# A GNN layer and a top-2 mixture of experts in one kernel: second dispatches deferred, slot loads paced, group 0 taken ahead in the opening

## What is computed

```python
def _L0_gnn_ref(x, adjacency, epsilon, W1, b1, rms_weight, W2, b2):
    neighbor_sum = jnp.einsum('bnm,bmd->bnd', adjacency, x)
    agg = epsilon * x + neighbor_sum
    h = jnp.einsum('bnd,dh->bnh', agg, W1) + b1          # H = 512
    h = jax.nn.silu(_rmsnorm(h, rms_weight))
    return jnp.einsum('bnh,hd->bnd', h, W2) + b2

def _L0_ffn_ref(x, Wg, bg, W1, b1, W2, b2):              # E = 8 experts, H = 512
    top_w, top_i = jax.lax.top_k(xf @ Wg + bg, 2)
    top_w = jax.nn.softmax(top_w, axis=-1)
    ...
    for e in range(E):
        h = jax.nn.gelu(xf @ W1[e] + b1[e], approximate=False)
        out = out + w_dense[:, e:e + 1] * (h @ W2[e] + b2[e])

x = x + _L0_gnn_ref(_layernorm(x), adj, ...)
x = x + _L0_ffn_ref(_layernorm(x), ...)
```

## Time and profile before

| | |
|---|---|
| runs | 565.95 us median (565.26 to 566.77) |
| profiled execution | 568.35 us, span 566.4 us, mean granted clock 0.934 |
| TensorE busy | 488.4 us (86%) |
| GpSimd busy | 361.7 us (64%) |
| VectorE busy | 354.4 us (63%) |
| ScalarE busy | 262.8 us (46%) |

### The profile page before, as it was taken

How to read it: one execution, slowest core, us unless ns; L and a number is a source line. 1 busy time by engine, 2 the same in 40 slices (tenths; PEclk the granted TensorE clock), 3 DMA queues, 4 the chain that set the end, 5 groups by cost and what they waited for, 6 DMA issues and landing times. The chain is left out here.

```text
span 566.4 us, 14003 instructions
## 1 busy us (share of the span) xinstructions
PE 488.4 (86%) x3693; PEld 437.6 (77%) x3693; DVE 354.4 (63%) x1486; ACT 262.8 (46%) x812; POOL 361.7 (64%) x334
## 2 busy tenths in 40 slices
PE   2589889999899998555718999999999999999993
PEld 1467677777677776455618999999999999999993
DVE  6647777666666766226424666767676767676762
ACT  0214123222222332114305777777777777777771
POOL 2323478887788786663473545454556888888886
PEclk9959789999998998977777999999999999999997
DMA  7971122222222221330122222322223555555531
GB/s 251 367 232 29 28 62 69 73 72 72 64 62 64 65 71 35 78 87 16 37 74 72 78 74 86 98 71 65 73 57 51 70 68 73 68 77 74 70 34 14
DMA packets 54577, 45.01 MB, mean 79 GB/s; under 512 B 9522, under 2 KB 46040, under 8 KB 54503
## 3 DMA queue, kind: packets, MB, share of 16 engines
q1 hardware_dynamic: 36480, 26.11, 16.9%
q0 software_dynamic: 16592, 17.13, 15.4%
q10 hardware_dynamic: 1430, 0.88, 0.6%
HBM read 25.75 MB, written 19.25 MB: 79 GB/s over the span
## 5 line engine op out<-in xcount | busy, mean ns | idle before, releaser
L663 ACT ACTIVATE gelu_t<-ps,block_w 128x128 f32<-128x128 f32 x568 | 163.0, 369 | 44.6 <-PE ps L566 25.4
L566 PE MATMUL ps<-slot_t,block_w 128*128 128x128 f32 x1136 | 154.8, 280 | 19.1 <-issue 13.7
L566 PEld LDWEIGHTS ps<-slot_t,block_w 128*128 128x128 f32 x1136 | 141.7, 196 | 20.6 <-issue 14.4
L376 POOL DMA_INDIRECT dispatched_rows<-payload,row_idx x128 | 127.0, 992 | 42.2 <-issue 35.7
L581 PE MATMUL ps<-experts,gelu_t 128*128 x1136 | 152.4, 278 | 0.5 <-ACT gelu_t L663 0.3
L581 PEld LDWEIGHTS ps<-experts,gelu_t 128*128 128x128 f32 x1136 | 140.1, 194 | 1.2 <-issue 1.1
L411 POOL DMA_INDIRECT out_y<-y_out,slot_rows x71 | 112.9, 1590 | 24.2 <-issue 21.3
L408 POOL DMA_INDIRECT out_y<-y_out,slot_rows x71 | 69.7, 982 | 66.2 <-issue 52.3
L942 DVE TENSOR_TENSOR y_bias<-ps,block_w 128x128 f32<-128x128 f32 x142 | 41.5, 292 | 98.3 <-issue 43.4
L930 DVE COPY block_w<-experts 128x644 f32 x142 | 71.1, 501 | 1.4 <-issue 1.3
L498 PE MATMUL ps<-w2e,hidden 128*128 128x136 f32 x512 | 71.8, 291 | 0.0
(11 more groups left out here) (135 smaller groups left out, 453.5 us busy)
## 6 DMA issues: line engine op xcount, KB each, us to landing
slot_rows<-dispatched_rows SPq DMA_DIRECT2D x142, 66.5 KB
xs<-in_x SPq DMA_DIRECT2D x16, 256.0 KB, 6.9
xs_t<-in_x_t SPq DMA_DIRECT2D x16, 256.0 KB, 7.1
experts<-in_f_w SPq DMA_DIRECT2D x16, 256.0 KB, 5.2
out_y<-y_out,slot_rows POOLq DMA_INDIRECT x142
adj_in<-in_adj_t SPq DMA_DIRECT2D x16, 128.0 KB, 6.3
dispatched_rows<-payload,row_idx POOLq DMA_INDIRECT x128
dispatched_rows<-pad_rows SPq DMA_DIRECT2D x18, 66.5 KB
```

Of the source, the lines that this page charges most:

```text
L376: pool.indirect_dma_start(rows[k], bass.IndirectOffsetOnAxis(row_idx[:, g, j * TOP_K + k:j * TOP_K + k + 1], 0), payload[:, g * JT + j, 0: ...
L566: mm = pe.matmul(bank((2 * i + c // 2) % FH_BANKS, c % 2 * SLOTS, SLOTS), block_w[:, i % BLOCKS, c * P:(c + 1) * P], slot_t[:, i % 2, :], ...
L663: act.activation(gelu_t[:, i % 2, c, :], ps[:, (2 * i + c // 2) % FH_BANKS, c % 2 * SLOTS:(c % 2 + 1) * SLOTS], ACT.Gelu, bias=block_w[:, ...
```

## The change

- GpSimd dispatches only the rows of the first expert (k = 0) in their step. Of the second expert's 64 dispatches, two a step follow one group later (`dispatch_second`), 30 in all; the other 34 stand between the first 60 tile writes. They have a semaphore of their own, for which SP waits before load 71.
- SP's first 16 slot loads wait for the 48 early k = 0 dispatches alone, and each for a mark of progress: of the last two groups (0 to 5) or of the slot norms (6 to 15). A pad follows each of the loads 16 to 31.
- TensorE's steps before 0 are written out anew: group 0's aggregation and quadratic form, the set-ups, spread(0), aggregate(2), and then step 0 with group 1's quadratic form and sums inside it, spread(1), quadratic(2) and sum_squares(2) behind it.
- In every step `prefix(s - 1)` moves behind the last `second_layer`.
- epsilon is the first load of ScalarE; a Silu on one column runs ahead of its loop; norm1(0) stands ahead of the W1 operations, setup_w2 behind scale_agg(0); the gate's set-up product uses PSUM bank 4 instead of 1.

```diff
@@ SP
+            def pad(g):
+                end = sp.value_load(region_end[0:1, g:g + 1], min_val=0, max_val=DUMMY - SLOTS)
+                sp.dma_start(rows[g // E][bass.ds(end, SLOTS), :], pad_rows[:]).then_inc(padded, 16)
...
-            sp.wait_ge(early_dispatched, 16 * JT * TOP_K * EARLY_GROUPS)
+            sp.wait_ge(early_dispatched, 16 * JT * EARLY_GROUPS)
             for i in range(RING):
+                if i < 4:
+                    sp.wait_ge((h_done, h_done, prefix_done, l2_done)[i],
+                               (C * (G - 2) + 1, C * (G - 1), G - 2, G - 1)[i])
+                elif i < 6:
+                    sp.wait_ge(h_done, (C * (G - 1) + 1, C * G)[i - 4])
+                else:
+                    sp.wait_ge(slots_normed, i - 5)
                 load_slots(i)
             sp.wait_ge(ends_ready, 1)
-            pad(0)
             for i in range(RING, EARLY):
                 load_slots(i)
-            pad(1)
+                if i - RING < KE:
+                    pad(i - RING)
...
-            sp.wait_ge(late_dispatched, 16 * JT * TOP_K * (G - EARLY_GROUPS))
-            for i in range(EARLY, NT):
+            sp.wait_ge(late_dispatched, 16 * JT * (G - EARLY_GROUPS))
+            for i in range(EARLY, TILES):
+                load_slots(i)
+            sp.wait_ge(second_dispatched, 16 * JT * G)
+            for i in range(TILES, NT):
                 load_slots(i)
@@ GpSimd
                 if live(s - 1):
                     pow_ln2(s - 1)
                 if live(s - 2):
-                    dispatch(s - 2, (0, 1))
+                    dispatch(s - 2, 0, 0)
+                    dispatch(s - 2, 1, 0)
+                if live(s - 3):
+                    dispatch_second(2 * (s - 3))
                 for g in STATS_AT.get(s, ()):
                     pow_ln1(g)
                 if live(s + 2):
                     pow_rms(s + 2)
                 if live(s - 2):
-                    dispatch(s - 2, (2, 3))
+                    dispatch(s - 2, 2, 0)
+                    dispatch(s - 2, 3, 0)
+                if live(s - 3):
+                    dispatch_second(2 * (s - 3) + 1)
             for i in range(NT):
...
+                write_tile(i)
+                done = 2 * (G - 1)
+                left, until = G * JT - done, TILES - 11
+                if i < until and (i + 1) * left // until > i * left // until:
+                    dispatch_second(done + i * left // until)
@@ TensorE
+            aggregate(0)
+            setup_quad()
+            quadratic(0)
+            aggregate(1)
+            setup_turns()
+            sum_squares(0)
+            setup_gate()
+            spread(0)
+            aggregate(2)
+            for s in range(G):
+                first_layer(s, (0, 1))
+                if s == 0:
+                    quadratic(1)
+                elif live(s + 1):
                     spread(s + 1)
+                first_layer(s, (2, 3))
+                if s > 0 and live(s + 2):
                     quadratic(s + 2)
...
+                residual(s, 0)
+                residual(s, 1)
+                second_layer(s, 0)
+                second_layer(s, 1)
+                if s == 0:
+                    sum_squares(1)
+                elif live(s + 2):
                     sum_squares(s + 2)
+                residual(s, 2)
+                second_layer(s, 2)
+                residual(s, 3)
+                second_layer(s, 3).then_inc(l2_done, 1)
                 if live(s - 1):
                     prefix(s - 1)
                 if live(s + 3):
                     aggregate(s + 3)
+                if s == 0:
+                    spread(1)
+                    quadratic(2)
+                    sum_squares(2)
@@ ScalarE
+            act.dma_start(eps_col[:], epsilon.to_broadcast([P, 1])).then_inc(eps_loaded, 16)
...
             act.wait_ge(pool_consts, 2)
+            act.activation(table_warm[:], ones[:, 0:1], ACT.Silu)
@@ VectorE, setup_w1
                 place_adj(0)
+                norm1(0)
                 dve.wait_ge(w1_loaded, 32)
```

More of the change, by code:

```diff
@@ L68, in moe_gnn @@
     AHEAD = 4
-    assert D == P and C == 4 and G > 8 and SLOTS == P
+    assert EARLY >= RING + KE and D == P and C == 4 and G > 8 and SLOTS == P
     with ExitStack() as ctx:
@@ L85, in moe_gnn @@
         before = sb("before", [P, P], BF16)
+        table_warm = sb("table_warm", [P, 1])
         neg_half = sb("neg_half", [P, JT])
@@ L370, in pow_rms, with dispatch, dispatch_second, write_tile @@
                                    ALU.pow).then_inc(rrms_ready, 1)
-            def dispatch(g, tiles):
-                pool.wait_ge(rows_ready, g + 1)
[L374 to L379, removed]
+            def dispatch(g, j, k):
+                if k == 1:
+                    signal = second_dispatched
+                else:
+                    signal = early_dispatched if g < EARLY_GROUPS else late_dispatched
+                pool.wait_ge(rows_ready, g + 1)
+                pool.indirect_dma_start(
+                    rows[k], bass.IndirectOffsetOnAxis(row_idx[:, g, j * TOP_K + k:j * TOP_K + k + 1], 0),
+                    payload[:, g * JT + j, 0:WID], None).then_inc(signal, 16)
+            def dispatch_second(n):
+                if n < G * JT:
+                    dispatch(n // JT, n % JT, 1)
+            def write_tile(i):
+                r = i % RING
+                pool.wait_ge(y_ready, i + 1)
+                token = bass.IndirectOffsetOnAxis(slot_rows[:, r, TOKEN:TOKEN + 1].bitcast(I32), 0)
+                if i < TILES:
+                    pool.indirect_dma_start(out, token, y_out[:, r, :], None, bounds_check=T - 1,
+                                            oob_is_err=False).then_inc(added[r], 16)
+                else:
+                    pool.indirect_dma_start(out, token, y_out[:, r, :], None, bounds_check=T - 1,
+                                            oob_is_err=False, compute_op=ALU.add).then_inc(added[r], 16)
             for s in range(-4, G + 2):
@@ L444, in setup_gate @@
                 for c in range(C):
-                    pe.matmul(bank(1, c * E, E), w2_t[:, c, :], ident_wg[:, P:ZW], start=True, stop=True)
-                pe.matmul(bank(1, C * E, E), b2_rows[:], ident_wg[:, P:ZW],
+                    pe.matmul(bank(4, c * E, E), w2_t[:, c, :], ident_wg[:, P:ZW], start=True, stop=True)
+                pe.matmul(bank(4, C * E, E), b2_rows[:], ident_wg[:, P:ZW],
                           start=True, stop=True).then_inc(setup_pe, 1)
@@ L518, in _ @@
             pe.matmul(bank(0, 0, H), ones[:], w1g, start=True, stop=True).then_inc(setup_pe, 1)
-            for s in range(-3, G):
-                if s == -2:
-                    setup_quad()
-                if live(s):
-                    if s == 0:
-                        pe.wait_ge(setup_dve, 9)
-                    first_layer(s, (0, 1))
-                if live(s + 1):
+            aggregate(0)
[3 more added lines that the diff above has]
+            setup_turns()
@@ L534, in _ @@
[L534 to L547 removed]
+                if s == 0:
+                    pe.wait_ge(setup_dve, 9)
@@ L898, in _ @@
             for s in range(-4, G):
-                if s == 0:
-                    setup_w2()
                 if live(s - 1):
                     second_norm(s - 1)
-                if live(s + 3):
+                if live(s + 3) and s > -3:
                     norm1(s + 3)
@@ L906, in _ @@
                     scale_agg(s + 1)
+                if s == -1:
+                    setup_w2()
                 if live(s - 1):
```

44 lines of the change are left out of this document (6 added, 38 removed).

## The result

The changed kernel is slower: 601.68 us median (600.93 to 602.0, 4 runs) against 566.36 (565.26 to 567.6, 4 runs) in the same session, a ratio of 1.062 [1.059, 1.065]. The profiled execution took 600.93 us, its span is 598.7.

The account below looks back on a forecast made before the run. GpSimd's queue was taken to bound the group loop and the accumulating writes. Terms 215.8 + 39 + 136.2 + 137.5 gave a span of 528.5 us, 37.9 less than 566.4; forecast 528 us, own range 517 to 540.

Parts of the forecast that it names:

- Writes and dispatches mixed: First part of tile loop: 71 writes and 34 dispatches fill GpSimd for 133.7 us, 2.0 us a tile at first.
- group 15's first layer: End of group loop: reached at 215.8 us instead of 232.17, by -11.4 for the loop and -5.0 for the opening.
- to the first tile write: From the last group's first layer until GpSimd starts tile writes: 39 us, bounds 34.6 and 55.5.
- to the first accumulating write: First half of tile writes with the moved dispatches between them: 136.2 us, set by GpSimd's own time.
- to the end: From the first accumulating write to the kernel's end: 137.5 us, as before, GpSimd issuing without a wait.
- The passage: Between group loop and tile loop: paced loads and fewer dispatches remove most stops, 39 us to GpSimd's first tile write.
- Opening: Before the steady group loop: group 3's first layer at 77 to 78 instead of 82.87, -5 us, bounds -9 and +2.
- Group loop: Ten group steps: 11.7 us each against 12.84 with fewer dispatches and moved prefix, -11.4 us, bounds -13 and -3.
- Load 71: Tile loop: SP's slot load waiting for the last dispatch lands some 4 us before its y is wanted.
- The lock of the two engines: Tile loop rival: dispatches wait for VectorE's block copies, 34 x 0.489 = 17 us, total 545 us; chance 0.03.
- Slower: Tile loop rival: dispatches stop the other engines, 1.43 us each, 49 us for 34, total 577 us; chance 0.06.
- The stops stay: Passage rival: stops come from engines' first pass through new code, 55.5 us instead of 39, total 545; chance 0.2.

Follow-up runs that it names:

- opening-and-prefix version: Kernel before with the new opening and moved prefix alone, GpSimd and SP as before: 560.18 us (0.989) on a slower chip, 526.3 us (0.994) on a faster one.
- session 3: Repeat of the unaltered changed kernel against the kernel before, on another slower chip: 597.43 us, ratio 1.057.
- paired version: Kernel before, nothing added, first-half tile writes in pairs 1.28 us apart: 530.14 us (1.001) on a faster chip, 578.47 us (1.023) on a slower one.

## Why the prediction was wrong

**What failed.** The step "Writes and dispatches mixed". It added up GpSimd's own time and put the price of a dispatch in the tile loop at its 1.26 us on GpSimd, nothing for the others. In the four terms of the sum:

| term, us | predicted | result (slower chip) | faster chip |
|---|---|---|---|
| group 15's first layer | 215.8 | 217.7 | 216.7 |
| to the first tile write | 39 | 43.9 | 36.3 |
| to the first accumulating write | 136.2 | 198.2 | 142.3 |
| to the end | 137.5 | 138.8 | 138.7 |
| span | 528.5 | 598.7 | 534.0 |

62.0 of the 70.2 us lie in the third term. That it is the moved dispatches is shown by the run with them back in the loop; that it is their being DMAs, by powers against 16-row writes on one chip. The forecast's description (GpSimd never waits, 2.0 us a tile) is what the faster chip shows, but not the chip the kernel was measured on, where the earlier trace rows already had the warning: all engines but GpSimd stand while GpSimd issues.

**The passage.** The size was near and within its bounds (43.9 for 39), for the wrong reason. I put the stops down to SP's loads and GpSimd's dispatches together and expected pacing of the loads to remove most. Pacing gained at most 2 us; spacing dispatches, with SP's burst kept, brought tile 10 forward by 18.6 (between two slower chips). On a faster chip the opening-and-prefix version has the burst too (16 loads in 17.39 us), and no idle over 4.17 us. What shortened the passage in the changed kernel is, by the nearest comparison, its fewer dispatches, six a step for eight: up to group 15's row_idx it differs from the version with all eight in the loop by nothing else, and from group 15's first layer to there lie 35.9 us (39.7 in session 3) against 46.0. That comparison is between chips. Whether SP's loads must be there at all for the stops was not tested.

**Opening.** Forecast -5 us at group 3's first layer, measured 82.87 - 74.07 = 8.8, inside the bound of 9. Spread(2) came at 49.40, not 53: 27.40 for first_layer(0) was 1.5 us early, and VectorE reached product(2) at 42.30, not 46.1. The term was mis-sized by 3.8 us.

**Group loop.** Forecast 11.7 us a step, measured 12.0, with the idle before the prefix gone. From group 4's to group 14's first layer: 208.93 - 86.11 = 122.8 against 128.4, so -5.6 and not -11.4, inside the bound of -3. Half of the shortfall of 5.8 us is 12.0 for 11.7 in nine steps (2.9 us): an idle of 0.32 us before the quadratic form, waiting for agg_r (the row at 102.48), which wasn't there before. The other half (3.0 us) is the step of 14.66, with a 2.27 us idle at the same place, in which VectorE makes the early table. The kernel before has that step too: its 12.84 us are a mean of nine steps of 12.66 and one of 14.48 (208.82 to 223.30), and the forecast took it away with the rest. The two errors, of opening and loop, nearly cancel: 217.7 for 215.8.

**Load 71.** I had it land 4 us before "its y is wanted". It is wanted earlier, by the norm four tiles ahead, and GpSimd reaches the last dispatch late. On the faster chip this idle of 7.96 us is more than the term's whole excess (6.1). I did name the idle as a sign of error, but gave it no price. On the slower chip it is hardly there, since all are late alike: load 71 goes at 434.56, 3.2 us after the last dispatch, and TensorE's longest idle between tiles 60 and 76 is 1.63 us.

**The lock of the two engines.** The Trainium skill, "SBUF - State Buffer", section "SBUF: two separate sides", would have a dispatch between tiles wait for a block copy. I weighed this with writes of 977 to 982 ns "beside" copies of 485 to 491 ns, and that reading was wrong: in the kernel before none of the 50 block copies between tiles 10 and 60 overlaps a write, so it says nothing. In the changed kernel 21 of 50 overlap a GpSimd DMA, and there the trace agrees with the page in kind: the copy at 320.64, beside the write at 320.02, takes 0.68 us, and dispatches take up to 1317 ns (median 961). The size is small, 0.58 us in the mean for an overlapping copy against 0.49. It is not the cause of the stops: on the faster chip all 50 copies overlap (up to 0.68 us), without them. The low chance was right, its evidence wasn't.

**The rivals.** "Slower" was right in its mechanism, its place and nearly in its price: 1.43 us a dispatch, measured 1.39 (16 rows, slower against faster chip), and 62.0 / 34 = 1.8 in the result with all else in that term. It was given 0.06, on the argument that a hundred dispatches in the group loop go with idles of 1 us. The observation was right, the conclusion wasn't: the changed kernel's ten steps with 60 dispatches take 122.8 and 121.2 us on slower chips and 121.1 on a faster one, and no silu, copy or product starts late there. With 80 dispatches the ten steps of the kernel before take 128.4 us, and those of its variants on faster chips 122.1 to 122.8: at most 0.08 us a dispatch. The price of 1.4 us belongs to the tile loop, and the stops to it and the passage. What these have and the group loop hasn't is open. One difference is SP's own DMAs: 13 in the 122.8 us of the ten steps, 60 in the 146.8 us between tiles 10 and 60. That 1.43 and 1.39 agree so closely is partly luck, as 1.43 was one stop divided by eight dispatches. "The stops stay" is true in part (it is small beside the rest), but not its mechanism: the same code runs without long stops on the faster chips, and spacing the dispatches removes most of them on a slower one.

**Why slower even on the faster chip.** The kernel before takes 529 us there, and its variants with an unchanged passage have no idle over 2.61 us in it, so the passage has little to give. The changed kernel reaches tile 0 at 235.1, 9.4 us ahead of the opening-and-prefix version (244.5). At tile 60 it is 3.6 ahead, since GpSimd sets 2.0 us a tile for 1.9, and at tile 71 it is 7.6 behind, through load 71.

**What stays open.** Why a GpSimd DMA makes other engines start late on some chips and not on others, and in the tile loop but not in the group loop. The DMAs' own times, their rows and bytes are ruled out as the difference; what is between was not found. No run had the 34 DMAs issued by another engine, or SP's loads taken away beside them. Nor was the mixture tried with the last dispatch some ten tiles earlier, which should save the 8 us at load 71.

## What to carry to other kernels

Where all engines but one stand in a trace, suspect what the remaining one issues, and before moving such instructions into another stretch put idle copies of them there and time it: here the same DMA cost the others next to nothing in the group loop and, on a slower chip, more than its own time between the tiles. Measure on more than one chip. Moving GpSimd DMAs out of a loop is worth at most the loop's gap to the next engine (0.6 us a step here), and they must go where nobody waits closely: of this change, only the opening and the moved prefix are worth keeping (0.989 and 0.994 on the two sorts of chip). A ring's load is wanted when the first stage ahead reads it, not when the result is due.

## What the runs showed of the hardware

- The same kernel took 529 to 530 us in sessions on two chips and 564 to 567 us on three others and in the result's session. Most of the difference lies in the passage: from group 15's first layer to the y of tile 10 the kernel before takes 78.0 us in the result's session, and the paired version, which has the same passage, 45.5 on a faster chip.
- On the slower chips a further GpSimd indirect DMA between the tiles costs 1.4 us more than on a faster one, and 16 rows cost as much as 128; 34 GpSimd powers of 1.05 us cost 10.5 us there and 10.7 on a faster one. In the group loop of the changed kernel dispatches 1.3 us apart made nobody late (none of 60 starts by over 0.09 us).
- There, writes 1.28 us apart in pairs cost 0.4 us a pair against the same writes 1.9 us apart; on a faster chip they cost nothing.
- A block copy on VectorE that overlaps a GpSimd DMA takes up to 0.68 us instead of 0.49, and a dispatch up to 1.32 us instead of 0.96, on both sorts of chip.
